# Cross-attention and ternary FFN on one core: the first turns of the projection stage rearranged

## The reference

```python
def _layernorm(x, axis=-1, eps=1e-05):
    m = jnp.mean(x, axis=axis, keepdims=True)
    v = jnp.var(x, axis=axis, keepdims=True)
    return (x - m) / jnp.sqrt(v + eps)
...
        q = _split_heads(queries @ Wq, h)
        k = _split_heads(keys @ Wk, h)
...
    x = x + _L0_xattn_ref(_layernorm(x, axis=-1), ctx_1024, ctx_1024, ...)
    x = x + _L0_ffn_ref(_layernorm(x, axis=-1), ...)
    x = x + _L1_xattn_ref(_layernorm(x, axis=-1), ctx_1024, ctx_1024, ...)
    x = x + _L1_ffn_ref(_layernorm(x, axis=-1), ...)
```

## Time and profile before

| | us |
|---|---|
| median of 3 runs | 406.5 (406.21 to 407.29) |
| the profiled execution, whole time | 406.27 |
| its span in the trace | 404.6 |
| projection stage, from the start of the span to the first product of attention | 46.5 |

### The profile page before, as it was taken

How to read it: one execution, slowest core, us unless ns; L and a number is a source line. 1 busy time by engine, 2 the same in 40 slices (tenths; PEclk the granted TensorE clock), 3 DMA queues, 4 the chain that set the end, 5 groups by cost and what they waited for, 6 DMA issues and landing times.

```text
span 404.6 us, 9204 instructions
## 1 busy us (share of the span) xinstructions
PE 332.8 (82%) x3118; PEld 235.1 (58%) x3118; DVE 305.9 (76%) x1025; ACT 264.3 (65%) x567; POOL 183.8 (45%) x207
## 2 busy tenths in 40 slices
PE   2989789999999999922667877869887999999975
PEld 1767567776777777611444555546455666666642
DVE  2799746777898989677899899897346787778772
ACT  1566444466545545734878988988667888888732
POOL 1213500211212375228999899885105545554550
PEclk9999999999999999965899999989999999999999
DMA  7699998969553440000000000000001212221101
GB/s 238 214 291 270 251 253 224 253 137 269 119 122 81 122 62 3 1 0 0 2 1 2 0 2 1 2 0 0 2 12 29 41 42 40 54 53 42 26 27 39
DMA packets 43869, 33.68 MB, mean 83 GB/s; under 512 B 19888, under 2 KB 39728, under 8 KB 43696
## 3 DMA queue, kind: packets, MB, share of 16 engines
q1 hardware_dynamic: 43824, 33.11, 32.9%
HBM read 24.71 MB, written 8.39 MB: 82 GB/s over the span
## 4 chain that ended last, share of the span: by engine, by line
PE 53%; DVE 19%; issue 14%; ACT 8%; POOL 5%; DMA 1%; SPq 0%; POOLq 0%; DVEq 0%; ACTq 0%
PE PS L1250 5%; PE PS L1169 5%; PE PS L1486 4%; PE PS L1239 4%; DVE sm L745 4%; PE PS L1308 4%; PE PS L1472 4%; PE PS L1230 4%; PE PS L1229 4%; PE PS L1269 3%; PE PS L1445 2%; PE PS L1467 2%; ACT pT L1000 2%; DVE sm L717 2%; PE PS L1435 2%
## 5 line engine op out<-in xcount | busy, mean ns | idle before, releaser
L1000 ACT ACTIVATE pT<-PS 128x512 f32<-128x512 f32 x64 | 36.5, 596 | 48.3 <-PE PS L1230 47.9
L610 DVE TENSOR_REDUCE negm<-PS 128x4 bf16<-128x512 f32 x64 | 42.3, 684 | 13.0 <-PE PS L1239 12.8
L439 POOL TENSOR_TENSOR sm<-sm,mhalf 128x1 f32<-128x1 f32 x16 | 11.3, 708 | 81.1 <-DVE sm L642 81.1
L455 POOL TENSOR_TENSOR kst<-kst,rows 128x1024 f32<-128x1024 f32 x16 | 37.6, 2352 | 6.4 <-ACT kst L1068 6.2
L1115 ACT ACTIVATE lnT<-PS,Atok 128x128 f32<-128x128 f32 x128 | 36.3, 369 | 2.0 <-DVE lnb L853 0.8
L1348 PE MATMUL PS<-identf,w2f 128*128 128x128 f32 x128 | 19.2, 298 | 21.4 <-ACT w2f L1057 21.3
L1230 PE MATMUL PS<-identb,negm 128*128 128x128 bf16 x256 | 34.9, 220 | 0.0
L469 POOL TENSOR_TENSOR kst<-kst,rows 128x1024 f32<-128x1024 f32 x14 | 33.1, 2363 | 0.0
L1250 PE MATMUL PS<-pT,vx 128*32 128x128 f32 x512 | 27.1, 285 | 5.2 <-ACT pT L1000 5.2
L1348 PEld LDWEIGHTS PS<-identf,w2f 128*128 128x128 f32 x128 | 15.1, 151 | 26.0 <-ACT w2f L1057 20.6
L494 POOL TENSOR_TENSOR rr<-ms,mhalf 128x8 f32<-128x8 f32 x16 | 26.4, 1647 | 1.9 <-DVE ms L935 1.9
(11 more groups left out here) (222 smaller groups left out, 979.1 us busy)
## 6 DMA issues: line engine op xcount, KB each, us to landing
scr_q<-qpart SPq DMA_DIRECT2D x8, 384.0 KB, 3.3
scr_k<-kpart SPq DMA_DIRECT2D x8, 384.0 KB, 4.5
X<-in_x SPq DMA_DIRECT2D x8, 256.0 KB, 4.6
CTXT<-in_ctxT SPq DMA_DIRECT2D x8, 256.0 KB, 5.1
vx<-in_ctx SPq DMA_DIRECT2D x16, 128.0 KB, 3.0
out<-rest SPq DMA_DIRECT2D x16, 128.0 KB, 1.7
rows<-in_rows SPq DMA_DIRECT2D x1, 1544.0 KB, 8.4
qst<-scr_q SPq DMA_DIRECT2D x8, 192.0 KB, 4.4
```

What stands on the lines that cost most here:

```text
L455: gp.tensor_tensor(n2[q.slot], n2[q.slot], ln2g, ALU.mult).then_inc(b_g2, 1)
L610: v.tensor_reduce(negm[f.slot % 2][:, 4 * hg:4 * hg + 4], PS[:, 2 + hg % 2, :].rearrange("p (h k) -> p h k", h=4), AX_X, ALU.max, negate=T ...
L1000: s.activation(pT[:, hg, :], PS[:, hg % 2, :], ACT.Exp, scale=float(DH0) ** -0.5).then_inc(a_e, 1)
```

## The change

Rows and context of a group get a semaphore each: `p_x` now counts the rows alone, `p_c` the context. The DMA of `wqk` is split in two of 256 KB in pieces of 1 KB: the key half first with a semaphore of its own, then the query half. PE no longer waits for weights before its first instruction; it runs ten products of the identity with itself, whose result nothing reads, then waits for the key half, and the query half is waited for at Q(0). K(0) moves from turn 2 to turn 1, ahead of T(0). In turn 2 Q(0) moves ahead of T(1), and ACT's lnT(1) moves behind highQ(0). All later turns keep their order.

```diff
-                sp.dma_start(CTXT[:, :, cols_g], ctxT_v[:, :, cols_g]).then_inc(p_x[g], 16)
+                sp.dma_start(CTXT[:, :, cols_g], ctxT_v[:, :, cols_g]).then_inc(p_c[g], 16)
...
-            sp.dma_start(wqk[:], chunks(A["wqk"])).then_inc(s_wqk, 16)
+            sp.dma_start(wk, chunks(A["wqk"])[:, :, D:2 * D]).then_inc(s_wk, 16)
+            sp.dma_start(wq, chunks(A["wqk"])[:, :, 0:D]).then_inc(s_wqk, 16)
...
-                    dve.wait_ge(p_x[f.b], 32)
+                    dve.wait_ge(p_x[f.b], 16)
...
-                if f:
-                    act.wait_ge(p_tr, f.b + 1)
-                    done(act, p_q, f, -1)
-                    s.activation(lnT[f.slot % 2][:].rearrange("p c t -> p (c t)"), PS[:, f.slot % 2, :], ACT.Copy).then_inc(p_lnT, 1)
+                if f and f.b != 1:
+                    columns(f)
                 if b:
                     mid_q = high(1, p_q, 2, qpart)
+                    if f and f.b == 1:
+                        columns(f)
...
             pe.wait_ge(s_const, 1)
-            pe.wait_ge(s_wqk, 16)
+            for _ in range(10):
+
+                t.matmul(PS[:, 7, 0:128], identf[:], identf[:], start=True, stop=True)
+            pe.wait_ge(s_wk, 16)
...
+                if f and f.b == 0:
+                    keys(f)
+                elif b and b.b > 0:
+                    keys(b)
+                if f and f.b != 1:
+                    turned_rows(f)
+                if b:
+                    if b.b == 0:
+                        pe.wait_ge(s_wqk, 16)
                     pe.wait_ge(p_lnT, b.b + 1)
-                    project(wq, lambda kc: lnT[b.slot % 2][:, kc, :], 2, p_q)
+                    project(b, wq, lambda kc: lnT[b.slot % 2][:, kc, :], 2, p_q)
+                if f and f.b == 1:
+                    turned_rows(f)
```

More of the change, by code:

```diff
@@ L153, in build @@
         PS = ctx.enter_context(nc.psum_tensor("PS", [128, 8, 512], F32))
-        s_wqk = sem("qk_weights_loaded"); s_w = sem("other_weights_loaded")
+        s_wqk = sem("q_weights_loaded"); s_wk = sem("k_weights_loaded"); s_w = sem("other_weights_loaded")
         s_wvo = sem("vo_weights_loaded"); s_w12 = [sem(f"ffn_weights_loaded{i}") for i in range(2)]
@@ L163, in build @@
         p_x = [sem(f"p_x_loaded{i}") for i in range(NG)]
+        p_c = [sem(f"p_context_loaded{i}") for i in range(NG)]
         p_st = sem("p_stats_chain"); p_ve = sem("p_variance_ready"); p_rs = sem("p_rstd_ready")
@@ L959, in middle, with columns @@
                     s.activation(mid, rest[n][:].rearrange("p (j c t) -> p j c t", j=GP, c=KC), ACT.Copy).then_inc(p_mid, 1)
+                def columns(f):
+                    act.wait_ge(p_tr, f.b + 1)
+                    done(act, p_q, f, -1)
+                    s.activation(lnT[f.slot % 2][:].rearrange("p c t -> p (c t)"), PS[:, f.slot % 2, :], ACT.Copy).then_inc(p_lnT, 1)
                 if b:
@@ L1162, in _, with project @@
             pe.wait_ge(s_const, 1)
-            pe.wait_ge(s_wqk, 16)
+            for _ in range(10):
+                t.matmul(PS[:, 7, 0:128], identf[:], identf[:], start=True, stop=True)
+            pe.wait_ge(s_wk, 16)
             def turn_p(_st, f, b):
-                def project(w, rhs, bank, s_out):
+                def project(b, w, rhs, bank, s_out):
                     for oc in range(KC):
@@ L1171, in project, with keys, turned_rows @@
                     last.then_inc(s_out, 1)
-                if b:
-                    pe.wait_ge(p_x[b.b], 32)
+                def keys(b):
+                    pe.wait_ge(p_c[b.b], 16)
                     done(pe, p_rest, b, -1, 2)
-                    project(wk, lambda kc: CTXT[:, kc, bass.ds(b.b * GP * S, GP * S)], 4, p_k)
-                if f:
+                    project(b, wk, lambda kc: CTXT[:, kc, bass.ds(b.b * GP * S, GP * S)], 4, p_k)
+                def turned_rows(f):
                     pe.wait_ge(p_ln, f.b + 1)
```

## The result

The changed kernel takes 403.9 us (median of 4 runs, 403.48 to 404.18) against 406.89 for the kernel before in the same runs: a ratio of 0.9922, 95% interval 0.9901 to 0.9943. That is 3.2 us faster by the ratio; the forecast was 403.6. The profiled execution took 403.48 with a span of 401.8, 2.8 shorter than before in both.

The account below looks back on a forecast made before the run. The start of a fixed-latency projection loop, lnb(2), was taken to bound the kernel: -2.8 on the path and 0 for the rest, 406.27 - 2.8 = 403.5, put at 403.6. The eight-in-ten range was 402.6 to 405.4.

Parts of the forecast that it names:

- The bound: Projection is a loop of fixed latency, 4.48 us a turn; everything hangs on its start, lnb(2), at 15.86 before.
- Rows' own semaphore: Start of DVE's statistics: stats(0) at 3.71 instead of 5.01, lnb(0) 1.30 earlier; stats(1) released by rows, near 8.
- Products: PE's start: ten products from 1.83 end near 5.6, at 6.2 at the latest, cost nothing; K(0) takes 1.74, not 3.03.
- Key weights: Load of the key half, first of the split: lands at 6.3, between 6.3 and 7.9 possible.
- Order: First turns on PE and ACT: K(0) from 6.35, T(0) to 8.75, Q(0) at 9.45, highQ(0) at 11.25, 3.35 earlier.
- DVE's list decides: DVE's own list sets lnb(2) at 13.05 instead of 15.86, 2.8 earlier; PE's branch would give 12.5.
- SP and DMA: Loads move ahead about as much as the engines; third stack, read at 57.35 with margin 1.0, makes no new wait.
- the rival in which the gain is given back: Behind the projection: DMA moves ahead only 1 us, third stack comes late, 404.3; chance 0.13 for 405.3 to 407.5.
- The slower rival: Feed-forward stage: PE's clock, low until near 196, rises three turns later, +5.4, to 408.9; chance 0.06.

Follow-up runs that it names:

- Thirty products: The changed kernel with thirty unread products on PE instead of ten: median 408.46 us, ratio 1.0038 to the kernel before.
- The one with the feed-forward stage kept busy: The changed kernel with 61 unread bfloat16 products in PE's idle time at the start of the feed-forward stage: median 403.75 us, ratio 0.9926 to the kernel before.
- two parts alone: The kernel before with statistics waiting for rows alone (ratio 0.9992), and with only ten unread products ahead of the weights wait (1.0031).
- each of the four taken out of the whole: The changed kernel without products (0.9990), statistics awaiting rows and context (1.0017), both weights in one DMA (0.9980), old PE and ACT order (0.9976); ratios to kernel before.
- whole weights: The changed kernel with both weights in one DMA of 512 KB, as before: median 405.08 us, ratio 0.9980 to the kernel before.

## Why the prediction was right, step by step

- **The bound.** Right. The loop of 4.5 us stood as it was, and its start carried over whole: 2.80 at lnb(2), 2.80 at the end. Thirty products show the same with the other sign.
- **Rows' own semaphore.** stats(0) at 3.73 (forecast 3.71), stats(1) at 7.84 (about 7.9). Right, and right that stats(0) isn't what matters but stats(1).
- **Products.** The step that failed. I had the rise of the clock 3.2 us after PE's first work, from one sight of it, and the products over near 5.6, at 6.2 at the latest. The sight itself was misread: two of K(0)'s eight records at the upper level are 0.43 of its time, so with K(0) over at 12.16 the rise came at 11.7, 3.7 after the first work, which puts it at 5.5 and the end of the products near 5.9. They ended at 6.52, all twenty records at the lower level. The first record of K(0) started at 6.31, as forecast (6.35), but two of its records ran at the lower level too, and T(0) started at 8.44 instead of 8.1. Over the eleven traces with unread products the rise came at 4.8 to 11.3, for the same first product at 1.9. One sight of an event that moves between executions was taken for a duration. The price of nothing for the products was 0.4 too low in the profiled execution, where the weights had landed at 5.9, and right in those where the weights landed behind the products.
- **Key weights.** 6.3 forecast, 5.9 in the profile, 6.5 and 7.1 in others. The step between equal transfers was a fair middle; the spread of 1.2 between executions was missing.
- **Order.** T(0), the new wait for lnT(0) (0.78, forecast 0.7) and Q(0) came in the order said. Q(0) started at 9.82 instead of 9.45, of which some 0.3 is the clock in K(0). Then it took 1.96 instead of 1.74, since the 1.74 was read from a Q(0) that followed T(1) without a gap, and highQ(0) came at 11.82 instead of 11.25. K(1) was to be just covered, and was not quite: it ended at 13.95 and stands on the chain.
- **DVE's list decides.** A near miss. restK(0) came at 11.70 (11.8) and lnb(2) at 13.06 (13.05), but restQ(0) started 0.75 behind restK(0), not 0.64: it waited 0.1 for highQ(0), which started at 11.82. The text had said what such a wait would mean: PE's branch decided. With highQ(0) at the forecast 11.25, DVE's list would have given 12.95. The error in PE's branch, 0.57, was hidden up to the last 0.1 by the other branch, which is why the sum came out so well. That part is luck.
- **SP and DMA.** Right in that nothing waited for a stack, but narrowly so. The last load of the third stack was issued at 49.56, 2.5 earlier than before, and took 4.9 to land instead of 4.2; it landed near 54.5, and PE read the stack at 54.56. The margin was 0.1 instead of the 1.0 taken. In the changed kernel run again (issued at 49.46, 4.1 to landing) it was 1.0 again, and 1.2 with the start moved by 4.7. So the rival in which the gain is given back there was 0.1 away from showing in the profiled execution.
- **The slower rival.** Its place was wrong: the clock near 196 is hidden. Its mechanism, a level of the clock that changes at other moments in other executions, shows at the start and, in one execution, at the entry of attention, where 2 us were lost. Twelve runs of the changed kernel lie between 403.36 and 404.83 but for two of 405.96 and 407.20.

No version beat the changed kernel clearly. The one with the feed-forward stage kept busy has 403.75 against 403.9 and 404.0, within the intervals.

## What to carry to other kernels

Where branches in parallel meet, price a change at the meeting point, with every branch that arrives there: here it moved by 0.2 and 0.3 us with two parts alone, the second time by landings only, and each of the four taken out of the whole cost 1.1 to 2.2. A chain of waits names one branch, and says nothing of how close the next one is; in the kernel before, 1.3 us at its very head were worth 0.2. And before a clock, a landing or anything else that varies between executions goes into a sum as a number, look at more than one sight of it.

## What the runs showed of the hardware

- The granted clock column doesn't show the lower level before its first rise: it reads 1.00 from 8 to 9 us while records of 256 columns take 631 ns against 380. Later falls it does show, as 0.50.
- With the same first product at 1.9 and eight to thirty unread products, the first rise came near 4.8, 5.2, 5.6, 5.7, 7.0, 7.1, 7.6, 8.0, 10.7 and 11.3 in ten executions, by the lengths of the records. In the two latest PE had been idle for 0.65 and 1.84 us behind the products, before any rise. In an eleventh (whole weights) it was idle for 1.25, with the products all at the lower level and K(0) behind them all at the upper: there the rise fell into the idle time. So the idle time alone doesn't tell when the rise comes.
- A load of 256 KB, third in the queue, landed 4.1 to 5.3 us after its issue in executions with the same two loads ahead of it.
